# Running the first norm two tile steps and the q/k chain one tile step further ahead in a two-layer Swin block on one Trainium2 core

## The reference

```
x  -> layernorm -> roll -> windows -> q, k, v = x @ qkv_w + qkv_b        (12 heads of 16)
      softmax(q k^T * scale [+ bias + mask]) v -> @ proj_w -> roll back -> x = x + that
x  -> layernorm -> gelu(x @ fc1_w + b) @ fc2_w + b -> x = x + that       (768 hidden)
```

## Time and profile before

| | |
|---|---|
| median of 3 runs | 5052.86 us (5048.24 to 5064.25) |
| the profiled execution | 5027.64 us, its span 5025.9 us |
| granted PE clock, mean over the span | 0.973 |
| busy: PE, DVE, ACT, POOL | 4214.8, 3507.2, 2796.4, 3304.9 us |
| DMA transposes issued by SP | 4 kinds, 512 of each |
| 16 DMA engines, busy share of SP's queue | 44.4% |

### The profile page before, as it was taken

One profiled execution on the slowest core, in us unless ns is written; L12 is line 12 of the kernel. 1 busy time (PEld: TensorE's weight loads), 2 busy tenths in 40 slices (PEclk: granted clock), 3 DMA queues, 4 the chain that ended last, 5 costly groups with the idle time before them and its releaser, 6 DMA issues. The chain is left out here.

```text
span 5025.9 us, 210881 instructions
## 1 busy us (share of the span) xinstructions
PE 4214.8 (84%) x83792; PEld 3123.0 (62%) x83792; DVE 3507.2 (70%) x9081; ACT 2796.4 (56%) x5921; POOL 3304.9 (66%) x6254
## 2 busy tenths in 40 slices
PE   4888888888888888888888888888888888888887
PEld 3666666666666666666666666666666666666665
DVE  5777766776677776666776766666776766666775
ACT  1555555555555555555555555555565555555555
POOL 4666666666666666666666666666666666666665
PEclk9999999999999999999999999999999999999999
DMA  3444444444444544444444444444444444444443
GB/s 92 83 87 84 86 84 84 84 86 84 83 83 86 89 84 85 84 83 80 88 85 83 84 85 84 84 83 85 88 86 85 86 82 83 85 84 83 83 83 63
DMA packets 1560720, 422.84 MB, mean 84 GB/s; under 512 B 1457462, under 2 KB 1558202, under 8 KB 1559740
## 3 DMA queue, kind: packets, MB, share of 16 engines
q1 hardware_dynamic: 1559740, 409.35, 44.4%
HBM read 31.56 MB, written 25.17 MB: 11 GB/s over the span
## 5 line engine op out<-in xcount | busy, mean ns | idle before, releaser
L1090 POOL TENSOR_SCALAR os<-o_tok 128x192 f16<-128x192 f32 x512 | 179.9, 351 | 1121.7 <-DVE o_tok L930 1121.0
L596 PE MATMUL bank<-w_fc,hid 128*128 128x192 f16 x9216 | 875.2, 253 | 6.7 <-DVE hid L950 4.6
L452 PE MATMUL bank<-w_qkv,xt 128*128 128x384 f16 x2560 | 540.8, 345 | 393.6 <-DMA xt<-xs 391.8
L950 DVE TENSOR_TENSOR hid<-hid 128x512 f16<-128x512 f32 x768 | 583.7, 777 | 396.6 <-POOL hid L1122 355.4
L596 PEld LDWEIGHTS bank<-w_fc,hid 128*128 128x128 f16 x9216 | 805.1, 101 | 61.5 <-DVE v_blk L906 17.5
L694 ACT ACTIVATE v_blk<-bank 64x192 f16<-64x192 f32 x1024 | 334.9, 327 | 806.8 <-PE bank L483 801.0
L700 ACT ACTIVATE p_exp<-ps_t 128x768 f32<-128x768 f32 x512 | 413.3, 807 | 502.6 <-PE ps_t L541 500.4
L917 DVE TENSOR_TENSOR pt<-p_exp,pt 128x768 f16<-128x768 f32 x512 | 492.0, 961 | 276.3 <-ACT pt L705 276.3
L1122 POOL TENSOR_SCALAR hid<-hid 128x512 f16<-128x512 f32 x768 | 534.0, 703 | 156.3 <-ACT hid L713 154.5
L584 PE MATMUL ps_s<-ht,w_fc 128*128 128x512 f16 x2560 | 606.8, 385 | 31.0 <-issue 28.4
L912 DVE TENSOR_REDUCE smax<-ps_s 128x12 bf16<-128x768 f32 x512 | 480.8, 939 | 174.9 <-PE ps_s L508 172.0
(11 more groups left out here) (118 smaller groups left out, 8759.1 us busy)
## 6 DMA issues: line engine op xcount, KB each, us to landing
x_img<-in_x_dram SPq DMA_DIRECT2D x256, 96.0 KB, 2.9
out_dram<-y_img SPq DMA_DIRECT2D x256, 96.0 KB, 2.5
xt<-xs SPq DMA_TRANSPOSE x512, 2.7
qkt<-qk SPq DMA_TRANSPOSE x512, 4.0
ot<-os SPq DMA_TRANSPOSE x512
ht<-xs SPq DMA_TRANSPOSE x512, 2.9
stage<-in_L_conv_fc_w_dram SPq DMA_DIRECT2D x2, 384.0 KB, 4.2
stage<-in_L_conv_w_fc_dram SPq DMA_DIRECT2D x2, 384.0 KB, 3.8
```

The costliest lines, as they stand in the source:

```text
L452: last = mm(dst, blocks[:, blk, :], w[:, part, n0:n1], start=(i == 0), stop=(i == 4 and bias is None))
L596: mm(bank[:, 0:C], hid16[:, hs, m, tok], w_fc2[layer][:, ws, m, :], start=(m == 0 and i == 0), stop=False)
L950: v.tensor_tensor(hid16[:, 1, m, :], hid[:, u % 4, :], hid16[:, 0, m, :], ALU.subtract)\
```

## The change

The first norm of a tile runs two steps earlier on every engine of its chain (`statistics(s + 5, 0)`, `centre(s + 5)`, `scale(s + 5)`, `apply1(s + 4)`, `norm1_turn(s + 5)`, and the pixel side, `x_transpose(s + 6)`, `order_next(s + 10)`, loads at s + 9). The q/k chain runs one step earlier (`qk_product(s + 3)`, `qk_hi(s + 2)`, `qk_lo(s + 2)`, `set_mask(s + 2)`, `qk_turn(s + 3)`). So `xt` and `qkt` each have one more step between their DMA and the product that reads them. The ring of `xt` has 6 buffers instead of 4, those of `qk` and `qkt` 3 instead of 2, `x_new` and `x_tok` grow, and `p_exp` and `hid` move into tiles that only the weight set-up uses. A group of the second layer now follows 7 groups behind the same tiles' first layer, not 4 or less; first and second layer groups still alternate, apart from four at either end. The DMA semaphores are four for each kind, and `hidden(0)` waits for all four.

```diff
+XT, QK = 6, 3
-    order = [(0, 0, 0), (0, 0, 1)]
-    for image in range(1, IMAGES):
-        order += [(image, 0, 0), (image - 1, 1, 0), (image, 0, 1), (image - 1, 1, 1)]
+    order = [(0, 0, 0), (0, 0, 1), (1, 0, 0), (1, 0, 1)]
+    for image in range(2, IMAGES):
+        order += [(image - 2, 1, 0), (image, 0, 0), (image - 2, 1, 1), (image, 0, 1)]
...
-        xt = sb("xt", [128, 4, 3, TOK], F16)
+        xt = sb("xt", [128, XT, 3, TOK], F16)
...
-                if live(s + 3):
-                    norm1_turn(s + 3)
+                if live(s + 5):
+                    norm1_turn(s + 5)
                 if live(s - 3):
                     norm2_turn(s - 3)
-                if live(s + 2):
-                    qk_turn(s + 2)
-                if live(s + 7) and s + 7 >= TILES and visit(s + 7)[1] == 0 and visit(s + 7)[0] + 1 < IMAGES:
-                    ge("x_ordered", rank(s + 7) | 1)
-                    load(visit(s + 7)[0] + 1, visit(s + 7)[2])
+                if live(s + 3):
+                    qk_turn(s + 3)
+                if live(s + 9) and s + 9 >= TILES and visit(s + 9)[1] == 0 and visit(s + 9)[0] + 1 < IMAGES:
+                    ge("x_ordered", rank(s + 9) | 1)
+                    load(visit(s + 9)[0] + 1, visit(s + 9)[2])
...
-                        for n in (p * GROUP + GROUP - 2, p * GROUP + GROUP - 1):
+                        for n in range(p * GROUP, (p + 1) * GROUP):
                             landed(pe, "ht_in", n)
...
-                if live(s + 4) and visit(s + 4)[1] == 0:
-                    x_transpose(s + 4)
+                if live(s + 6) and visit(s + 6)[1] == 0:
+                    x_transpose(s + 6)
...
-                if live(s + 2):
-                    qk_product(s + 2)
+                if live(s + 3):
+                    qk_product(s + 3)
...
-                if live(s + 2):
-                    apply1(s + 2)
+                if live(s + 4):
+                    apply1(s + 4)
...
-                if live(s + 8) and visit(s + 8)[1] == 0 and s + 8 >= TILES:
-                    order_next(s + 8)
-                if live(s + 1):
-                    set_mask(s + 1)
+                if live(s + 10) and visit(s + 10)[1] == 0 and s + 10 >= TILES:
+                    order_next(s + 10)
+                if live(s + 2):
+                    set_mask(s + 2)
```

More of the change, by code:

```diff
@@ L68 @@
 SLABS = SIDE // WS
+XT, QK = 6, 3
 def group_order():
-    order = [(0, 0, 0), (0, 0, 1)]
-    for image in range(1, IMAGES):
-        order += [(image, 0, 0), (image - 1, 1, 0), (image, 0, 1), (image - 1, 1, 1)]
-    return order + [(IMAGES - 1, 1, 0), (IMAGES - 1, 1, 1)]
+    order = [(0, 0, 0), (0, 0, 1), (1, 0, 0), (1, 0, 1)]
+    for image in range(2, IMAGES):
+        order += [(image - 2, 1, 0), (image, 0, 0), (image - 2, 1, 1), (image, 0, 1)]
+    return order + [(image, 1, half) for image in (IMAGES - 2, IMAGES - 1) for half in range(2)]
 GROUPS = group_order()
@@ L230, in swin_program @@
         COUNT |= dict.fromkeys(("exp_loaded", "gelu_loaded"), PHASES)
-        COUNT |= dict.fromkeys(("centred", "rstd"), TOTAL + 6)
+        COUNT |= dict.fromkeys(("centred", "rstd"), TOTAL + 8)
         S = {name: sem(name) for name in COUNT}
-        LANDED = {name: [sem(f"{name}_even"), sem(f"{name}_odd")] for name in ("xt_in", "ht_in", "ot_in", "qkt_in")}
+        LANDED = {name: [sem(f"{name}{r}") for r in range(4)] for name in ("xt_in", "ht_in", "ot_in", "qkt_in")}
         x_loaded = [sem(f"x_loaded{h}") for h in range(2 * SLABS)]
@@ L244, in landed @@
             if n >= 0:
-                eng.wait_ge(LANDED[name][n % 2], 16 * (n // 2 + 1))
+                eng.wait_ge(LANDED[name][n % 4], 16 * (n // 4 + 1))
         def token_rows(n):
             image, _, t = visit(n)
-            return x_tok[:, image % 2 * TILES + t, :]
+            return x_tok[:, image % 3 * TILES + t, :]
         def stream(n, which):
-            _, layer, t = visit(n)
-            return token_rows(n) if layer else (x_new, x_mid)[which][:, t, :]
+            image, layer, t = visit(n)
+            if layer:
+                return token_rows(n)
+            return x_mid[:, t, :] if which else x_new[:, image % 2 * TILES + t, :]
         def live(n):
@@ L260, in run @@
         def run(slot):
-            for s in range(-4, TOTAL + GROUP + 10):
+            for s in range(-6, TOTAL + GROUP + 10):
                 slot(s)
@@ L470, in qk_product @@
                     landed(pe, "xt_in", n)
[L471 removed]
+                    contract(ps_qk[:, 0:2 * C], w_qkv[layer], xt[:, n % XT], 0, 2 * C, b_qk[layer][:, :])\
                         .then_inc(S["qk_mm"], 1)
@@ L508, in scores @@
                                 last = mm(ps_s[w * WIN:(w + 1) * WIN, par, g * WIN:(g + 1) * WIN],
-                                          qkt[rows, n % 2, g, tok], qkt[rows, n % 2, PAIRS + g, tok],
+                                          qkt[rows, n % QK, g, tok], qkt[rows, n % QK, PAIRS + g, tok],
                                           start=(layer == 1 and g == 0), stop=False, skip_group_check=True)
@@ L531, in scores_turned @@
                                 last = mm(ps_t[rows, g // 3, place:place + WIN],
-                                          qkt[rows, n % 2, PAIRS + g, tok], qkt[rows, n % 2, g, tok],
+                                          qkt[rows, n % QK, PAIRS + g, tok], qkt[rows, n % QK, g, tok],
                                           start=(layer == 1 and g % 3 == 0 and w == 0), stop=False, skip_group_check=True)
@@ L755, in slot @@
                     v_hi(s)
-                if live(s + 4) and visit(s + 4)[1] == 0:
-                    x_evac(s + 4)
+                if live(s + 6) and visit(s + 6)[1] == 0:
+                    x_evac(s + 6)
                 if mlp and place == 1:
@@ L896, in qk_lo @@
                         last = v.scalar_tensor_tensor(
-                            out=qk[:, n % 2, heads, place, :],
+                            out=qk[:, n % QK, heads, place, :],
                             in0=ps_qk[:, i * C:(i + 1) * C].rearrange("p (h d) -> p h d", d=HD), scalar=UNSCALE,
-                            in1=qk[:, n % 2, heads, 0, :], op0=ALU.mult, op1=ALU.subtract)
+                            in1=qk[:, n % QK, heads, 0, :], op0=ALU.mult, op1=ALU.subtract)
                     last.then_inc(S["qk_lo"], 1)
@@ L1032, in _ @@
             pool.wait_ge(made, 1)
-            for r in range(2):
+            for r in range(QK):
                 last = g_.tensor_scalar(qk[:, r, 0:HEADS, 3, 0:REGIONS],
```

76 lines of the change are left out of this document (38 added, 38 removed).

## The result

The changed kernel takes 4976.4 us (median of four runs, 4961.4 to 4978.6) against 5051.2 us (four runs, the one added being 5049.5). The ratio is 0.984, with a 95% interval of 0.9815 to 0.9867: 1.6% faster, 75 us. I had forecast 1% slower. The span of the profiled execution went from 5025.9 to 4976.8 us, so 49 of the 75 us can be looked for in the two traces. The other 26 are the distance of the profiled executions from their medians: the old kernel's was 24 us faster than its median, the new one's 2 us slower.

What follows compares the result with a forecast made beforehand. The prediction took the way by which ht comes, through SP's in-order issues, as the bound. Per phase -1.24 + 0.3 + 1.29 = +0.35 us, +44 us over 127 phases, plus 5 at the start: about 5100 us, range 4880 to 5220.

Steps and rivals of the forecast that it cites:

- The waits for xt and qkt: PE's waits for these transposes, 558.6 us in all, would go; a 3 to 5 us wait before each hidden product instead.
- A: The o_tok of place 1 in a phase; PE was to stand before hidden(0) 22.4 us after it, ht to land at 26.0.
- SP's row of issues as what is late: Nine DMA issues, 13.50 us, make ht late; only SP's own waiting between ot and ht goes, -1.24 us a phase.
- SP's total wait for POOL: Sign of being right: SP's wait for POOL's low part falls much below 1088.8 us.
- Loads and stores: On SP's way to ht, one DMA (1.00 us) more in first-layer phases, one less in second-layer ones; counted 0.
- The clock: PE's idle before hidden(0) lowers its clock, so the hidden product starts slowly; +1.29 us a phase on the mean.
- H to A: Piece of a phase from hidden(0) to the o_tok of place 1, 12.17 us; 13.60 us when begun at low clock.
- Landing of ht: Time from issuing ht to hidden(0), taken as 4.4 us against 4.1 and 4.2 before; +0.3 us a phase.
- The rivals: Clock stays high, chance 0.18; waits simply vanish, 0.13; SP's issues stretch, 0.09; nothing happens, 0.08.
- the SP term: ot to ht on SP at place 3 falls to 2.66 us, two back-to-back issues; -1.24 us a phase.
- The clock holds: Rival: PE's clock stays at 2.4 GHz despite the idle before hidden(0); -0.94 us a phase, 4939 us; chance 0.18.

Runs made afterwards that it cites:

- ht_ahead: Changed kernel, with SP issuing the ht transpose of place 3 ahead of the xt transpose instead of behind it; 4688.7 us, ratio 0.935 to the kernel before.
- moves_held: Changed kernel, with SP holding loads and stores of places 1 and 2 until after the qkt of place 3; 4747.4 us, ratio 0.942 to the kernel before.
- loads_at_7: Changed kernel, with SP's image loads put back two steps (tile s + 7 instead of s + 9); 4958.1 us, ratio 0.989 to the kernel before.
- fill_12: Changed kernel, with twelve extra 512-column matmuls on PE ahead of its wait for ht, result overwritten; 4750.7 us, ratio 0.947 to the kernel before.
- before_ht: Kernel before the change, with only the ht of place 3 issued ahead of the xt on SP; 5255.5 us, ratio 1.048 to the unedited kernel before.
- moves_and_ht: Changed kernel, with the edits of moves_held and ht_ahead together; 4531.6 us, ratio 0.900 to the kernel before.
- norm2_early: moves_and_ht, with POOL doing the second norm's low part of place 0 right behind apply1; 4504.6 us, ratio 0.898 to the kernel before.

## Why the prediction was wrong

**The waits for xt and qkt: right.** Both went, and came back as one wait for ht in every phase, 486.3 us where I said some 450. That these two numbers agree is partly luck: PE stood ready before hidden(0) at A + 20.5 us on the mean, not A + 22.4, and the product began at A + 24.3, not A + 26.0.

**SP's row of issues as what is late: right.** -1.24 us forecast, -1.1 measured, with no pause of SP left between ot and ht; ht_ahead and moves_held, which only change this row, move the time by 4 to 5 points. That SP's total wait for POOL would be much below 1088.8 us was wrong (1022.7). At place 3 the wait for norm1's low part did go, from 149.5 to 1.6 us, but 913 us of the total stood at places 0 and 1, and there it grew to 1018.

**Loads and stores: right in kind, too large.** +1.0 and -1.0 us forecast, +0.7 and -0.6 measured, with phases 1.5 us apart (forecast about 2), cancelling nearly (loads_at_7).

**The clock: right.** +1.29 forecast; H to A grew by 1.2 and 1.5 us, and fill_12 gave 1.47 back.

**Landing of ht: this step failed.** I took 4.17 and 4.09 us from the issue of ht to hidden(0) as its landing, and added 0.3. But that piece ends with whoever comes last. The trace of before had it in a row that I didn't read, the single ht issued at 2561.46:

```profile
L368 SPq DMA_TRANSPOSE ht<-xs x1: 2081/2081/2081, 2561.5 to 2561.5; - x1
...
DMA to landing us min/median/max: 3.2/3.2/3.2
```

It had landed at 2564.7, a microsecond before the hidden product. And neither hidden product of the earlier trace rows has a bracket of idle time before it: PE came to it with less than 0.15 us of pause. My two phases were also at the long end: over 98 phases the piece was 3.3 us, not 4.1. Of these, 2.8 were the landing (the 2.9 at the median of the earlier trace rows said the same) and 0.5 the time from the landing to the product. The 112 waits of 62.9 us that I took for PE's are those of the weight load; the matmul behind it waited 21 times, for 28.4 us. So "ht arrives about when PE does" was right, and ht did come last in half of the phases (before_ht), but its way was shorter than I had added it up.

In the changed kernel the piece is 2.6 us: a landing of 2.35, and 0.25 to the product, which now always waits. The term was -0.7 us where I had +0.3. The 1.0 us between them times 127 is 127 us, all of the distance from a forecast of +49 to the -49 of the profiled execution and some 30 more, which the SP term, the clock and the loads take back.

Of the 0.7 us, 0.25 are PE no longer coming after ht; that could have been read from the trace. The other 0.45 are a shorter landing, 2.82 to 2.35 us on the mean of the same 98 phases, and only part of it is explained. The landing is counted from the start of the issue, and the issue of ht itself held SP for 1.46 us on the mean before and 1.20 after: over 1.4 us in 37 of the 98 phases before, in one after. Why an issue takes longer at some times is not shown. The view of all ht in the changed kernel:

```profile
DMA to landing us min/median/max: 2.3/2.3/4.4
```

That PE stands still meanwhile is not why: in fill_12 PE is at work, and issue to start is 2.49 us. With ht ahead of xt the landing is longer than in the changed kernel (2.55 us on the mean in ht_ahead, 2.81 in moves_and_ht). What else is on the DMA engines at that moment may decide; no run took this apart.

**The rivals.** None was it. "The clock holds" gives nearly the right number (4939) by the wrong way: the clock didn't hold. With the piece read as what it was, and the landing left as it stood, the term would have been -0.25 instead of +0.3 and the forecast 5102 - 70 = 5032 us, just faster than before. The rest of the way to 4976 us is the shorter landing, which nothing in the trace of the kernel before foretold.

## What to carry to other kernels

Before a piece "from the issue of a DMA to its consumer" is used as the landing, look at who came last: the landing by itself, and whether the consumer had idle time in front of it. Where a consumer has none, its own way bounds or the two are level, and shortening the DMA's alone gives little or nothing. Where look-ahead takes waits away, they gather before the one input that could not be had sooner; reorder the issuing queue for that input after, not before, the look-ahead (-8.4 points with it, +5.1 without), and if a wait as long as those here (2.5 to 3.9 us on the mean) is left ahead of a long product, try cheap matmuls in it: here they kept the clock up.

## What was not expected of the hardware

Long waits of PE and a low clock go together, but not one for one. In the kernel before, the 18 waits of 2.7 us or more between 500 and 5002 us were all followed by a granted clock of 0.50 to 0.70 over the next 3.4 us; in 9 of them the clock was down when the matmuls began, in the other 9 it fell up to 1.3 us later. The wait of 4.6 us at 82.72 was followed by 1.00. In the changed kernel 95 of 98 hidden products started slowly, after waits of 1.41 us and more, and three did not, after 2.01, 2.22 and 2.62 us; in ht_ahead one of 2.61 us was followed by 3.69 us for the first ten matmuls, and one of 3.16 us by a start at full speed. Twelve extra matmuls of 512 columns in each of 128 phases, 1536 in all, make the program 187 us shorter.

Issuing a DMA transpose held SP for 1.18 us at best, with 1.33 between starts, and for up to 3.0 us in the changed kernel and 3.5 in the kernel before. Seven to ten such issues in a row take far longer than the landing of any one of them, and set the phase in the changed kernel and still in norm2_early.
